# A feed-forward stage with one tile of lookahead, its rounding on GpSimd and its norm on ScalarE

## What is computed

```python
def _act_quant(x):
    scale = 127.0 / jnp.clip(jnp.max(jnp.abs(x), axis=-1, keepdims=True), 1e-05)
    xq = jnp.clip(jnp.round(x * scale), -128.0, 127.0) / scale
    return x + jax.lax.stop_gradient(xq - x)
def _bitlinear(x, w):
    return jnp.einsum('bsi,oi->bso', _act_quant(x), _weight_quant(w))
gate = jax.nn.silu(_bitlinear(x, w_gate))
up = _bitlinear(x, w_up)
ffn = _bitlinear(gate * up, w_down)
...
x = x + _L0_xattn_ref(_layernorm(x, axis=-1), ctx, ctx, ...)
x = x + _L0_attn_ref(_layernorm(x, axis=-1), ...)
x = x + _L0_ffn_ref(_layernorm(x, axis=-1), w_gate, w_up, w_down)
```

## Time and profile before

| what | value |
|---|---|
| median of 3 runs | 958.99 us (954.76 to 959.69) |
| the profiled execution, its own time | 959.17 us |
| its span, first to last instruction | 957.4 us |
| mean granted TensorE clock | 0.988 |
| busy, share of the span: PE, DVE, ACT, POOL | 94%, 82%, 72%, 36% |
| DMA, mean over the span | 33 GB/s |

### The profile page before, as it was taken

How to read it: one execution, slowest core, us unless ns; L and a number is a source line. 1 busy time by engine, 2 the same in 40 slices (tenths; PEclk the granted TensorE clock), 3 DMA queues, 4 the chain that set the end, 5 groups by cost and what they waited for, 6 DMA issues and landing times. The chain is left out here.

```text
span 957.4 us, 29217 instructions
## 1 busy us (share of the span) xinstructions
PE 896.8 (94%) x9714; PEld 726.8 (76%) x9730; DVE 788.0 (82%) x1711; ACT 689.3 (72%) x1983; POOL 343.2 (36%) x487
## 2 busy tenths in 40 slices
PE   5999999999999999999999988999999996999997
PEld 4788888888888888888888876777777773555554
DVE  3778878888888888878878868888888886999997
ACT  3677776777767777677776756776777665988887
POOL 1322223222232222333323237566666631222221
PEclk9999999999999999999999989999999997999999
DMA  8111111111111111111111000000000000000001
GB/s 301 36 38 39 44 39 34 40 39 44 38 33 38 39 44 38 33 38 39 44 38 34 21 1 2 1 2 0 1 0 1 2 1 1 28 28 28 28 28 39
DMA packets 31618, 31.64 MB, mean 33 GB/s; under 512 B 3280, under 2 KB 30800, under 8 KB 31568
## 3 DMA queue, kind: packets, MB, share of 16 engines
q1 hardware_dynamic: 30720, 30.73, 10.4%
q10 hardware_dynamic: 848, 0.33, 0.1%
HBM read 26.86 MB, written 4.19 MB: 32 GB/s over the span
## 5 line engine op out<-in xcount | busy, mean ns | idle before, releaser
L485 ACT ACTIVATE probs<-psum,nmax 128x256 f32<-128x256 f32 x512 | 237.2, 487 | 89.5 <-DVE nmax L445 89.5
L445 DVE TENSOR_REDUCE nmax<-psum 128x2 f32<-128x512 f32 x256 | 158.9, 683 | 30.2 <-PE psum L315 30.2
L328 PE MATMUL psum<-id_sb,probs 128*128 128x128 f32 x1024 | 137.2, 278 | 14.1 <-ACT probs L485 14.0
L328 PEld LDWEIGHTS psum<-id_sb,probs 128*128 128x128 f32 x1024 | 113.0, 142 | 29.8 <-ACT probs L485 28.3
L493 POOL TENSOR_TENSOR rstd<-vare,minus_half 128x1 f32<-128x1 f32 x96 | 52.7, 549 | 199.8 <-DVE vare L382 197.3
L502 POOL TENSOR_TENSOR cl<-c_sb,ch 128x512 fp32r<-128x512 f32 x64 | 81.5, 1274 | 99.8 <-ACT ch L460 99.8
L485 ACT ACTIVATION_READ_ACCUMULATOR probs<-psum,nmax 128x1 f32 x512 | 112.4, 219 | 0.0
L466 ACT ACTIVATE probsT<-psum 128x512 f32<-128x512 f32 x160 | 90.8, 621 | 11.4 <-PE psum L328 11.4
L509 POOL TENSOR_TENSOR rm<-rinv,hm_sb 128x256 f32<-128x256 f32 x64 | 39.7, 620 | 127.6 <-DVE rinv L421 127.6
L315 PE MATMUL psum<-k_sb,qb 32*128 32x256 f32 x1024 | 78.5, 403 | 0.0
L1006 PE MATMUL psum<-wb_all,xqT 128*128 128x512 bf16 x240 | 66.4, 391 | 10.4 <-DVE probs L906 7.1
(11 more groups left out here) (126 smaller groups left out, 2304.6 us busy)
## 6 DMA issues: line engine op xcount, KB each, us to landing
c_sb<-in_ctx_t SPq DMA_DIRECT2D x64, 256.0 KB, 2.7
x_sb<-in_x SPq DMA_DIRECT2D x32, 128.0 KB, 2.0
out<-y_sb SPq DMA_DIRECT2D x32, 128.0 KB, 1.7
w_all<-in_w_gate SPq DMA_DIRECT2D x1, 1024.0 KB, 7.7
w_all<-in_w_up SPq DMA_DIRECT2D x1, 1024.0 KB, 9.8
w_all<-in_w_down SPq DMA_DIRECT2D x1, 1024.0 KB, 12.3
wqkv_sb<-in_w_qkv SPq DMA_DIRECT2D x1, 768.0 KB, 6.6
wq_sb<-in_wq ACTq DMA_DIRECT2D x1, 256.0 KB, 3.7
```

The costliest lines, as they stand in the source:

```text
L328: last = nc.tensor.transpose(sp[g][:, c:c + P], probs[:, 2 * g + u, kh * P:(kh + 1) * P], id_sb[:])
L445: nc.vector.tensor_reduce(nmax[:, 2 * g:2 * g + 2], sp[g].rearrange("p (u s) -> p u s", u=2), AX.X, ALU.max, negate=True).then_inc(max_don ...
L485: nc.scalar.activation(probs[:, j, :], sp[g][:, u * S:(u + 1) * S], ACT.Exp, bias=nmax[:, j:j + 1], accum_out=rsum[:, j:j + 1]).then_inc(e ...
```

## The change

In the feed-forward stage:

- xn is made on ACT, as rstd x + (-mean rstd) in one activation (Identity with a scale and a bias per partition). POOL makes the bias in two more instructions, nmean and nmr.
- hq, the rounding of the inner rows, goes from ACT to POOL, behind fd, and fd now waits for hscale.
- y_sb is made in two steps: ACT scales the product out of PSUM (`act_down`), POOL adds the residual (`pool_fin`).
- gate and up run one tile ahead in place of two. The body of DVE becomes hmax, hmaxc, hscale(t), amax, amaxc, ascale(t+2), stat and mv(t+3), hid(t+1). That of ACT: hqT(t-1), xqT(t+1), xn(t+2), silu(t+1), xq(t+2), y(t-1). PE: turn xq(t+1), down(t-1), gate and up(t+1), turn hq(t). POOL: fd and hq(t), fgu(t+2), the add(t-1), nmean, vare, rstd and nmr(t+3).
- The loops of ACT and POOL in this stage are written out rather than looped.

```diff
-        def dve_fin(v, t, par):
-            v.wait_ge(down_mm, t + 1)
-            v.wait_ge(fd_done, t + 1)
-            v.wait_ge(out_done[par], t * 8 - 8 * par)
-            nc.vector.scalar_tensor_tensor(y_sb[par][:], d_ps, fd[par][:, 0:1], at(t), ALU.mult,
-                                           ALU.add).then_inc(fin_done, 1)
+        def act_down(a, t, par):
+            a.wait_ge(down_mm, t + 1)
+            a.wait_ge(fd_done, t + 1)
+            a.wait_ge(out_done[par], t * 8 - 8 * par)
+            nc.scalar.activation(y_sb[par][:], d_ps, ACT.Copy, scale=fd[par][:, 0:1]).then_inc(dn_done, 1)
+
+        def pool_fin(p, t, par):
+            p.wait_ge(dn_done, t + 1)
+            nc.gpsimd.tensor_tensor(y_sb[par][:], y_sb[par][:], at(t), ALU.add).then_inc(fin_done, 1)
...
+        def pool_shift3(p, t):
+
+            p.wait_ge(xn3_done, t)
+            p.wait_ge(stats3, t * 3 + 2)
+            nc.gpsimd.tensor_tensor(nmean[:], mv[:, 0:1], minus_one[:], ALU.mult)\
+              .then_inc(nmean_done, 1)
+            pool_rstd3(p, t)
+            p.wait_ge(nmean_done, t - 1)
+            p.wait_ge(rstd3_done, t + 1)
+            nc.gpsimd.tensor_tensor(nmr[:], nmean[:], rstd[:], ALU.mult).then_inc(nmr_done, 1)
+
+        def act_xn3(a, t):
+            a.wait_ge(nmr_done, t - 1)
+            a.wait_ge(aq, t * 3 - 2)
+            a.wait_ge(xs_done, t)
+            nc.scalar.activation(xn[:], at(t), ACT.Identity, bias=nmr[:, 0:1],
+                                 scale=rstd[:, 0:1]).then_inc(xn3_done, 1)
...
-        def pool_fd(p, t, par):
-            p.wait_ge(hqs, t * 3 + 2)
+        def pool_fd_h(p, t, par):
+
+
+            p.wait_ge(hqs, t * 3 + 3)
             if not isinstance(t, int) or t > 1:
-                p.wait_ge(fin_done, t - 1)
+                p.wait_ge(dn_done, t - 1)
+                p.wait_ge(ht_mm, t * 2 - 2)
             nc.gpsimd.tensor_tensor(fd[par][:], hmaxc[:], w_mean[:, 2:3],
                                     ALU.mult).then_inc(fd_done, 1)
+            nc.gpsimd.tensor_scalar(hq[par][:], hid[par], hscale[:, 0:1], ROUND, ALU.mult,
+                                    ALU.add).then_inc(hs_done, 1)
...
-        def act_scale_h(a, t, par):
-            a.wait_ge(hqs, t * 3 + 3)
-            if not isinstance(t, int) or t > 1:
-                a.wait_ge(ht_mm, t * 2 - 2)
-            nc.scalar.activation(hq[par][:], hid[par], ACT.Copy, bias=ROUND,
-                                 scale=hscale[:, 0:1]).then_inc(hs_done, 1)
...
         def pe_down(pe, t):
-            pe.wait_ge(fin_done, t)
+            pe.wait_ge(dn_done, t)
...
+                def body(t, par):
                     dve_hmax(v, t, par)
...
                     dve_unit_h(v, t)
                     dve_scale_h(v, t)
...
+                    if t + 2 < NT:
+                        dve_absmax_x(v, t + 2)
+                        dve_scale_x(v, t + 2)
+                    if t + 3 < NT:
+                        dve_mean(v, LN3, t + 3, at(t + 3))
+                    if t + 1 < NT:
                         dve_hid(v, t + 1, 1 - par)
```

More of the change, by code:

```diff
@@ L71, in block_kernel @@
         eps_col = sb("eps_col", [P, 1])
+        minus_one = sb("minus_one", [P, 1])
+        nmean = sb("nmean", [P, 1])
+        nmr = sb("nmr", [P, 1])
         wq_sb = sb("wq_sb", [P, KT, D])
@@ L856, in block_kernel @@
         xn3_done = sem("xn3_done")
+        nmean_done = sem("nmean_done")
+        nmr_done = sem("nmr_done")
         aq = sem("aq")
@@ L871, in block_kernel @@
         down_mm = sem("down_mm")
+        dn_done = sem("dn_done")
         fin_done = sem("fin_done")
@@ L1178, in _ @@
                 nc.vector.memset(eps_col[:], EPS).then_inc(const_set, 1)
+                nc.vector.memset(minus_one[:], -1.0).then_inc(const_set, 1)
                 dve_stats(v, LN1, 0, x_sb[:], (x_in, 16))
@@ L1466, in _, with body @@
                 pe_gate_up(pe, 0)
[L1467 to L1472, removed]
+                def body(t, par, ahead1=True):
+                    if ahead1:
+                        pe_xq(pe, t + 1)
                     if not isinstance(t, int) or t > 0:
                         pe_down(pe, t - 1)
-                    if ahead2:
-                        pe_gate_up(pe, t + 2)
+                    if ahead1:
+                        pe_gate_up(pe, t + 1)
                     pe_ht(pe, t, par)
@@ L1483, in _ @@
                     body(n * 2 + 1, 1)
-                body(NT - 2, 0, ahead2=False)
-                body(NT - 1, 1, ahead2=False)
+                body(NT - 2, 0)
+                body(NT - 1, 1, ahead1=False)
                 pe_down(pe, NT - 1)
@@ L1490, in _ @@
                 v.wait_ge(y2_ev, NT)
-                dve_quant_x(v, 2)
+                dve_mean(v, LN3, 2, at(2))
                 dve_hid(v, 0, 0)
-                def body(t, par, ahead3=True, ahead1=True):
+                def body(t, par):
                     dve_hmax(v, t, par)
-                    if ahead3:
-                        dve_mean(v, LN3, t + 3, at(t + 3))
                     dve_unit_h(v, t)
                     dve_scale_h(v, t)
-                    if ahead1:
-                        dve_hid(v, t + 1, 1 - par)
[L1502 to L1512, removed]
-                    body(t, t % 2)
[L1514 to L1518, removed]
+                    if t + 2 < NT:
[4 more added lines that the diff above has]
+                    if t + 1 < NT:
+                        dve_hid(v, t + 1, 1 - par)
+                for t in range(NT):
+                    body(t, t % 2)
             @block.scalar
@@ L1522, in _ @@
                 act_silu(a, 0, 0)
[L1523 to L1527, removed]
-                        act_scale_x(a, t + 2)
[L1529 to L1543, removed]
+                def body(t, par):
+                    if t > 0:
+                        act_ht(a, t - 1)
+                    if t + 1 < NT:
+                        act_xqt(a, t + 1)
+                    if t + 2 < NT:
+                        act_xn3(a, t + 2)
+                    if t + 1 < NT:
+                        act_silu(a, t + 1, 1 - par)
+                    if t + 2 < NT:
+                        act_scale_x(a, t + 2)
+                    if t > 0:
+                        act_down(a, t - 1, 1 - par)
@@ L1544, in _, with body @@
+                for t in range(NT):
+                    body(t, t % 2)
                 act_ht(a, NT - 1)
+                act_down(a, NT - 1, 1)
             @block.gpsimd
             def _(p):
-                pool_rstd3(p, 2)
-                def body(t, par, ahead3=True, ahead2=True):
-                    if ahead2:
+                pool_shift3(p, 2)
+                def body(t, par):
+                    pool_fd_h(p, t, par)
+                    if t + 2 < NT:
                         pool_fgu(p, t + 2, par)
-                    if ahead3:
-                        pool_rstd3(p, t + 3)
-                    pool_fd(p, t, par)
@@ L1557, in _ @@
[L1557 to L1565, removed]
+                    if t > 0:
+                        pool_fin(p, t - 1, 1 - par)
+                    if t + 3 < NT:
+                        pool_shift3(p, t + 3)
@@ L1568 @@
+                for t in range(NT):
+                    body(t, t % 2)
+                pool_fin(p, NT - 1, 1)
 _NAMES = ["x", "ctx_t", "wq", "bq", "wk", "bk", "wv", "bv", "wo", "bo", "w_qkv", "b_qk", "b_v2", "w_out",
```

## The result

The changed kernel takes 960.78 us (median of 20 runs, 958.26 to 964.66) against 958.98 us for the kernel before (20 runs beside them): a ratio of 1.0023, 95% interval [1.0013, 1.0032]. A second set of 12 runs gave 1.0018 [1.0005, 1.0030]. Its profiled execution took 959.81 us with a span of 957.7.

The account below looks back on a forecast made before the run. An ACT and POOL loop at 4.54 us per tile was to replace DVE's 4.65 as the bound: 28 steps give -3.1 us, the stage's edges +2.3, so -0.8 and 958.4 us, range 953 to 965.

Parts of the forecast that it names:

- the bound before: Feed-forward stage of the kernel before: DVE has no time of its own left, 4.65 us per tile.
- The circle of ACT and POOL: Once per tile: xn, silus, xq, y, add, nmean, vare, rstd, nmr, back to xn; 4.54 us, the bound after.
- ACT's wait ahead of xn: Sign expected in the profile after: ACT waits for POOL's nmr ahead of xn; without it the once-per-tile loop was wrong.
- Loop 2: Two tiles around through hq on POOL: (7.4 + h)/2 per tile, h being hq's time; 4.22 us, hidden.
- the price of hq: Time of hq's 1024 columns on POOL: 1.04 us taken, with 1.90 and 2.35 kept for the rivals.
- Rival A: POOL's rounding hq costs as two-input work and the two-tile loop binds: 963.2 to 970 us; chance 0.22.
- B: Rival: the ACT and POOL loop is shorter than summed; at a step of 4.30, 951.7 us; chance 0.18.
- loop 1: ACT and POOL, once per tile, from xn through y, add and nmr to the next xn: eleven terms, 4.54 us.
- C: Rival: DVE stretches POOL's work; with add, xn and y at upper bounds 4.76 us per tile, 964.6; chance 0.16.
- The edges: Start and finish of the feed-forward stage: last two steps, end after the last hmax, first step; together +2.3 us.
- drain: Last two hmax-to-hmax steps: 3.12 and 3.55 us before, 8.45 together after, so 1.8 us more.
- first step: First hmax-to-hmax step: about 0.4 us shorter, since DVE reaches hid of tile 1 without xn or y_sb between.

Follow-up runs that it names:

- y_split_only: Kernel before with y_sb split into y on ACT behind the silus and the add on POOL; lookahead, xn and hq stay: 952.35 us, ratio 0.9932.
- add_last: Changed kernel with POOL's residual add of tile t-1 moved behind nmean, vare, rstd and nmr of tile t+3: 953.61 us, ratio 0.9956 to before.
- small_dose: Changed kernel with one extra one-column POOL instruction, whose output nothing reads, behind each residual add: 962.47 us, ratio 1.0046 to before.
- hq_first: Changed kernel with POOL's add moved behind the norm of tile t+3, and fd behind hq instead of ahead: 952.19 us, ratio 0.9939 to before.
- before_unrolled: Kernel before with only the feed-forward loops of ACT and POOL written out, same instructions in the same order: 957.32 us, ratio 0.9998.
- busy_pe: Changed kernel with 12 transposes that nothing reads added on PE ahead of the last tile's transposes: 960.36 us, ratio 1.0016 to before.
- last_y_on_dve: Changed kernel with y of the very last tile made by DVE in one instruction: 960.72 us, ratio 1.0021 to before.
- short_tail: hq_first with, for the last tile only, hq in halves on ACT and POOL and y by DVE in one instruction: 950.72 us, ratio 0.9909 to before.
- hq_only: Kernel before with only hq moved from ACT to POOL behind fd; lookahead of two, xn and y stay: 974.27 us, ratio 1.0152.
- hq_halves: Kernel before with hq split: columns 0 to 511 on ACT, 512 to 1023 on POOL behind fd: 960.14 us, ratio 1.0018.
- y_and_halves: Kernel before with the edits of y_split_only and hq_halves together, and the last y on DVE: 952.56 us, ratio 0.9930.

## Why the prediction was wrong

**Right: the bound before and the bound after.** DVE's fullness before is shown by y_split_only: 0.40 us off DVE, and the step falls by 0.26, to what DVE's order then takes. The circle of ACT and POOL is shown by add_last (the add's 0.69 leaves the circle, and the step falls to the next loop) and by small_dose (0.13 us more on an engine that is idle for 30% of the time comes on top of every step). ACT's wait ahead of xn, named as the sign, is there in every tile. Loop 2 behind it is shown by hq_first, where fd's 0.16 counts half; its rate is 4.28 without fd, and 4.35 with it, where the prediction had 4.22 for h = 1.04; with the measured h of 1.12 its formula gives 4.26.

**Right: the price of hq.** 1.12 us on POOL against 1.04, between the bounds and at their low end; one stream of columns costs (1.12 - 0.19)/1024 = 0.91 ns each, where the prediction took half of kbd's 1.67 ns for two. The Trainium skill, GPSIMD Engine Reference, section "Engine selection", calls one-input work there roughly line rate; the trace agrees (1.12 us for 1024 columns, where kbd's two operands take 1.90). Rival A, which needed 2.0, falls. So does B: loop 1 came out longer than the sum, not shorter. C falls for the changed kernel: the add takes 0.73 there.

**The step that failed is the sum of loop 1, by its size.** 4.54 was forecast, 4.61 is the measured step. Two terms are off: xn holds the next instruction on ACT 0.51 us, not 0.42 (it takes 0.60; the row of xq stood for it, with 0.51 named as the upper bound), and nmr starts 0.69 after rstd, not 0.63. That is 0.15 too little; the rest is within 0.03 each and gives 0.08 back, so that the sum came as close as it did partly by luck. Over 28 steps 0.07 is 2.0 us. Against it stands that before's steps average 4.67, not the 4.65 of the prediction, 0.7 us in all, since two of them took 4.93 and 5.00. So the steps gained 1.64 us where 3.1 were forecast, less than the edges cost: a small gain turned into a small loss. y's price of 0.47 and the add's of 0.69 were exact.

**The edges** were sized +2.3 and came out at +2.4: drain 2.0 for 1.8, end 0.98 for 0.9, first step -0.55 for -0.4. Here the reasoning held: with one tile of lookahead the end of the work no longer runs faster than its middle. The drain was 0.2 larger and the first step 0.15 shorter than forecast, and the two errors nearly cancel.

**What stays open.** The forecast was 0.6 us under before and the result is 1.8 over: 2.4 us. The stage accounts for 1.6 of them (-0.8 forecast, +0.8 measured). Another 0.3 lies outside the span: the changed kernel's time is 2.1 us longer than its span in every run, before's 1.8. That 0.3 is not from the written-out loops (before_unrolled 1.8). It is there in add_last, hq_first and busy_pe too, is 0.1 in last_y_on_dve and short_tail and nothing in small_dose, which points at what comes last on the engines; but y_split_only, which also ends with POOL's add, has 1.8, and hq_only and hq_halves, which end on DVE, have 2.0. Its cause is open. Stage and span together give 1.1 us against 1.8 between the medians; the first interval (1.2 to 3.1 us) lies just over 1.1, the second (0.5 to 2.9) holds it. Whether the clock at the end adds to it is not settled.

**Where the gain went.** The parts alone give 0.9932 (y), 1.0152 (hq) and 1.0101 (xn). The change takes them together: with xn off DVE, hq on POOL no longer lengthens any instruction of DVE in this stage (amax beside it takes 0.42 as before), and with hq off ACT, xn no longer stands behind it there. The gain of y went to the order on POOL, where the add was put ahead of the norm of three tiles on, and to the lookahead, which costs 2 us in the drain. With two swaps in POOL's order (the norm ahead of the add, hq ahead of fd) the same parts give 0.9939, and with a shorter tail 0.9909 and 0.9906, 8.7 to 9.0 us under before.

## What to carry to other kernels

When work is taken off the full engine and spread over others, write down the circle that the new handoffs close, by the order of each program: a small instruction behind a wait on an engine that is idle for 30% of the time can be on it, and swapping two calls was worth more here (6.4 us) than the whole change. On POOL, ask of each wait what stands behind it and who needs that first. A sum of eleven terms that leaves a gain of 0.11 us per tile is no gain yet: here the one operation without a row of its own form was off by 0.09.

## What the runs showed of the hardware

DVE's tensor_scalar from SBUF to SBUF, 256 columns of fp32, was held up while POOL ran hq: 0.88 us in place of 0.41 in hq_only, its end 0.15 to 0.16 behind POOL's in hq_only, hq_halves and y_and_halves. Other DVE instructions beside hq kept their durations: in the changed kernel amax (0.42) and amaxc, a tensor_scalar of one column (0.15), in hq_only hid (1.28). An activation (Identity) with a bias and a scale per partition took 0.60 us on 256 columns from SBUF where one (Copy) with only the scale per partition took 0.51. The granted clock, once at 1.00, fell to 0.57 to 0.60 in single stretches of 4 us near the beginning (add_last) and at the end of the stage (add_last, last_y_on_dve), where PE had just waited 1.8 to 2.0 us; after the same wait of 1.8 us it stayed at 1.00 in the profiled executions of the changed kernel and of hq_first.
